# Adding half of each token's expert results by accumulating transfers instead of by VectorE

## The reference

```python
probs = softmax(xt @ w_router)                     # T = 2048 tokens, E = 16 experts
top_w, top_i = top_k(probs, 4)                     # each token has 4 experts
g = silu(xt @ we1) * (xt @ we3)                    # per expert, H = 128
moe_out = sum over the token's 4 experts of  weight * (g @ we2)
shared = silu(xt @ ws1) * (xt @ ws3) @ ws2         # for every token, HS = 512
out = shared / 5 + moe_out * (4 / 5)
x = x + gb * out
```

## Time and profile before

| | us |
|---|---|
| runs | 423.79, 425.45, 425.90; median 425.45 |
| the profiled execution | 426.04 |
| its span (first to last recorded instruction) | 424.3 |
| PE busy | 351.2 (83%) |
| DVE busy | 273.0 (64%) |
| ACT busy | 199.6 (47%) |
| POOL busy | 237.5 (56%) |
| mean granted TensorE clock | 0.92 |

### The profile page before, as it was taken

The page is one execution under the profiler, slowest core; times in us unless marked ns, Lnnn a source line. Parts: engine busy times, 40 slices in busy tenths (PEclk is TensorE's granted clock), DMA queues, the critical chain, the costliest instruction groups (busy, mean ns, idle before and its releaser), DMA issues.

```text
span 424.3 us, 8354 instructions
## 1 busy us (share of the span) xinstructions
PE 351.2 (83%) x2372; PEld 317.7 (75%) x2372; DVE 273.0 (64%) x732; ACT 199.6 (47%) x437; POOL 237.5 (56%) x328
## 2 busy tenths in 40 slices
PE   3988999975999996796655989989999899897552
PEld 1777899974999985675654878878888798786542
DVE  1878988879897564267885554545544455258577
ACT  2446777643657446246351554545545455332020
POOL 1486996546888787877770355655655556600000
PEclk9979999987799998799686999999999999999685
DMA  7154400000011239952223465555546653289411
GB/s 239 59 206 140 131 14 25 14 12 3 15 43 58 85 104 333 355 194 97 99 104 94 127 187 152 151 150 151 174 133 174 171 135 117 87 317 411 177 43 57
DMA packets 54732, 56.65 MB, mean 134 GB/s; under 512 B 17440, under 2 KB 47008, under 8 KB 54688
## 3 DMA queue, kind: packets, MB, share of 16 engines
q1 hardware_dynamic: 46688, 34.34, 27.6%
q0 software_dynamic: 6912, 19.93, 12.5%
q10 hardware_dynamic: 1088, 1.84, 1.3%
HBM read 31.56 MB, written 24.53 MB: 132 GB/s over the span
## 4 chain that ended last, share of the span: by engine, by line
PE 46%; DVE 20%; issue 12%; POOL 11%; ACT 7%; DMA 2%; SPq 1%; DVEq 0%; ACTq 0%; POOLq 0%
PE ps L1408 13%; PE ps L1410 11%; PE ps L1409 11%; POOL xg_rows L551 9%; ACT xT_hi L805 2%; PE ps L1730 2%; DVE y_in L1191 2%; PE ps L1760 2%; DVE gT_lo L1356 2%; DVE act_g L1154 2%; ACT g_hi L674 1%; PE ps L1415 1%; DVE g_lo L1161 1%; POOL hrow L536 1%; DVE xT_lo L1349 1%
## 5 line engine op out<-in xcount | busy, mean ns | idle before, releaser
L578 POOL DMA_INDIRECT y_rows<-y_sb,dest x80 | 76.7, 959 | 72.1 <-ACT y_sb L830 57.6
L551 POOL DMA_INDIRECT xg_rows<-hrow,slot_u x64 | 67.1, 1049 | 19.0 <-issue 17.9
L1408 PE MATMUL ps<-rpool 128*128 128x256 f32 (+3 forms) x228 | 71.7, 314 | 6.5 <-DVE rpool L1232 4.5
L1409 PE MATMUL ps<-rpool 128*128 128x256 f32 (+3 forms) x228 | 68.5, 300 | 0.0
L1410 PE MATMUL ps<-rpool 128*128 128x256 f32 (+3 forms) x228 | 68.4, 300 | 0.0
L1349 DVE TENSOR_TENSOR xT_lo<-ps,xT_hi 128x512 fp32r<-128x512 f32 x40 | 27.7, 692 | 41.9 <-ACT xT_hi L805 41.9
L1408 PEld LDWEIGHTS ps<-rpool 128*128 128x128 f32 x228 | 46.4, 203 | 8.7 <-DVE rpool L1232 4.7
L1408 PE MATMUL ps<-w_hi_routed,xT_hi 128*128 x160 | 49.5, 309 | 4.0 <-issue 4.0
L1409 PEld LDWEIGHTS ps<-rpool 128*128 128x128 f32 x228 | 46.5, 204 | 0.5
L1410 PEld LDWEIGHTS ps<-rpool 128*128 128x128 f32 x228 | 46.2, 203 | 0.6
L1409 PE MATMUL ps<-w_lo_routed,xT_hi 128*128 x160 | 45.7, 286 | 0.0
(11 more groups left out here) (208 smaller groups left out, 963.0 us busy)
## 6 DMA issues: line engine op xcount, KB each, us to landing
xs<-xg_rows SPq DMA_DIRECT2D x80, 128.0 KB
y_in<-y_rows SPq DMA_DIRECT2D x8, 1024.0 KB, 13.3
w_raw_routed<-in_L_ffn_we_dram SPq DMA_DIRECT2D x4, 768.0 KB, 9.3
xg_rows<-empty SPq DMA_DIRECT2D x1, 2304.0 KB, 8.2
x_in<-in_L_attn_x_dram SPq DMA_DIRECT2D x16, 128.0 KB, 2.4
out_dram<-x SPq DMA_DIRECT2D x16, 128.0 KB, 1.8
wmod_sb<-in_L_wmod_dram ACTq DMA_DIRECT2D x3, 512.0 KB, 6.9
w_raw_routed<-in_L_ffn_we_dram SPq DMA_DIRECT2D x1, 1536.0 KB, 14.2
```

The source lines that it names most:

```text
L551: nc.gpsimd.indirect_dma_start(out=xg, out_offset=bass.IndirectOffsetOnAxis(ap=slot_u[:, t, k:k + 1].bitcast(U32), axis=0), in_=hrow[:, t, ...
L578: nc.gpsimd.indirect_dma_start(out=yb, out_offset=bass.IndirectOffsetOnAxis(ap=dest[:, r, i:i + 1].bitcast(U32), axis=0), in_=y_sb[:, r, i ...
L1408: nc.tensor.matmul(dst, w[0], x_[0], start=first, stop=False)
L1409: nc.tensor.matmul(dst, w[0], x_[1], start=False, stop=False)
```

## The change

```diff
-        s_yin = [sem(f"y_in{b}") for b in range(NB)]
+        s_yin, s_yacc = ([sem(f"{n}{b}") for b in range(NB)] for n in ("y_in", "y_added"))
@@ SP's queue
-                    sp.dma_start(y_in[b][:, rows], yb[first:first + BT // 2 * P * TOPK, :].rearrange(
-                        "(t p k) d -> p t k d", p=P, k=TOPK)).then_inc(s_yin[b], 16)
+                    sp.dma_start(y_in[b][:, rows, 0:2], yb[first:first + BT // 2 * P * TOPK, :].rearrange(
+                        "(t p k) d -> p t k d", p=P, k=TOPK)[:, :, 0:2]).then_inc(s_yin[b], 16)
@@ GpSimd's queue, behind the last scatter
+            for r in range(RING):
+                pool.wait_ge(s_back[r], 32 * (NPAIR // RING))
+            for b in SUM_ORDER:
+                pool.wait_ge(s_yin[b], 32)
+                for half in range(2):
+                    first = 1 + (b * BT + half * BT // 2) * P * TOPK
+                    rows = slice(half * BT // 2, (half + 1) * BT // 2)
+                    nc.gpsimd.dma_start(y_in[b][:, rows, 0:2], yb[first:first + BT // 2 * P * TOPK, :].rearrange(
+                        "(t p k) d -> p t k d", p=P, k=TOPK)[:, :, 2:4], accum_op=ALU.add).then_inc(s_yacc[b], 16)
@@ VectorE's queue, add_rows(b)
-                dve.wait_ge(s_yin[b], 32)
-                then(nc.vector.tensor_tensor(y[:, :, 0:2, :], y[:, :, 0:2, :], y[:, :, 2:4, :], ALU.add))
-                summed()
+                dve.wait_ge(s_yacc[b], 32)
                 then(nc.vector.tensor_tensor(y[:, :, 0, :], y[:, :, 0, :], y[:, :, 1, :], ALU.add))
```

## The result

The changed kernel is slower: 432.45 us median of 8 runs (428.25 to 435.48) against 425.49 of 8 runs of the kernel before in the same comparison. The ratio is 1.0138 with a 95% interval of 1.0104 to 1.0173, which on 425.45 us is +5.9 us (+4.4 to +7.4). So it lost 1.4%, clear of the noise and still under 2%. The two profiled executions took 431.37 and 426.04 us, +5.3.

A forecast was written before the change was run, and what follows sets the result against it. VectorE was taken as the bound. Block 0's late rows put unit 11 8.0 us later, three savings of 2.31 give back 6.9, and the clock takes part: +2.75, 428.2 us (428.8 profiled), likeliest case 425.0 to 431.4, overall 421 to 440.

The forecast's parts named there:

- the likeliest case: An accumulating transfer costs two copies and block 0 comes late: middle +2.75 us, range 425.0 to 431.4 us, 44 in 100.
- the rival of three movements: Accumulating costs three or more movements, or GpSimd issues slower than 4.1 us each: 431.5 to 443.5 us, 30 in 100.
- What goes: On VectorE after the last scatter: addition L1191 goes, four times 2.285 us, 2.31 with the small gap behind it.
- Block 0 has no slack: Before the change block 0 was complete at 379.8 us, just as VectorE asked for it at 379.9.
- Two copies for one accumulating transfer: On the DMA engines: two reads for one write count as two copies, 3.0 us for 512 KB.
- The share of the engines: Beside other loads block 0's two accumulating transfers get half to two thirds of the DMA engines, taking 12 or 9 us.
- GpSimd's first addition moves about 1 us later: After block 0's loads land at 377.45 us, GpSimd's first accumulating transfer begins moving at 378.45.
- The clock: TensorE's clock falls before down(11); if it holds or falls at later gaps, block 3's L1202 comes +1.1 or +4.4 us.
- accumulating is nearly a copy: Rival: an accumulating transfer takes 1.5 us per 512 KB; middle -2.4 us, 423.0, break-even about 2.2 us; 26 in 100.
- -8.9: Floor of the change if no rows ever came late and TensorE's clock holds: 416.6 us, practically excluded.

The follow-up runs named there:

- e1: The changed kernel with GpSimd's eight accumulating transfers made plain copies that nobody adds (result incomplete); ratio 1.0044 to before, stage 53.7 us.
- e5: The changed kernel with accumulating transfers for block 0 alone, the other blocks loaded whole and added by VectorE; ratio 1.0304 to before, stage 63.7 us.
- e4: The changed kernel with SP's loads of blocks 2, 1 and 3 held until block 0's accumulating transfers landed; ratio 1.0218 to before, stage 61.7 us.
- e2: The kernel before without VectorE's addition L1191, rows 2 and 3 loaded but left out of the sum; ratio 0.9880, stage 45.8 us.
- e3: The changed kernel with accumulating transfers for blocks 1 and 3 alone, blocks 0 and 2 loaded whole; ratio 0.9957 to before, stage 48.2 us.
- e7: The changed kernel in block order 2, 0, 1, 3, block 2 loaded whole and added by VectorE, the others accumulating; ratio 0.9884 to before, stage 47.1 us.
- e8: Block order 2, 0, 1, 3, block 2 whole, the others accumulating, plus unread matmuls in TensorE's two gaps; ratio 0.9855 to the kernel before, stage 45.6 us.
- e6: The changed kernel with 36, 14 and 10 unread matmuls in TensorE's three gaps; ratio 1.0056 to the kernel before, stage 53.9 us.

## Why the prediction was nearly right

Forecast were 428.8 us for an execution like the profiled one, +2.75; measured were 431.37, and in spans +5.1. The direction and the way of the loss were right, the size was about half of it. The median of 432.45 lies 1 us above the range of the likeliest case (425.0 to 431.4), inside the range of 421 to 440 that covers the rivals as well, and by the number alone it would fit the rival of three movements. What decides between them are the waits and the rates. Taken step by step:

- **What goes** was right: 9.1 us less on VectorE, and at blocks 2, 1 and 3 nothing new was waited for.
- **Block 0 has no slack** was right and decides. Its rows were asked for at +10 and came at +22.3 (forecast 390.2 - 369.87 = +20.3).
- **Two copies for one accumulating transfer** was nearly right. In GB/s it is 208 against 365 for loads in the windows of the result and 385 for e1's copies, a factor of 1.8 to 1.9; 512 KB at 208 GB/s take 2.5 us, not 3.0, against 1.4 for a load. That the pairs landed at about 397, 403 and 409 us (forecast 398.5, 404.5 and 410.5) is partly luck: from block 0's to block 2's it took 5.1 us, and then about 6 a pair because `out`'s stores ran beside them (0.44 of the 1.38 MB that moved between 400 and 406 us).
- **The share of the engines** was put between a half and two thirds, middle taken. From the windows it is (365 - 263) / (365 - 208) = 0.65 for the accumulating side. The rule cited from the Trainium skill, "DMA: Bandwidth & Descriptors", section "Queues, rings and completion order", of turns packet by packet, gives two thirds if such a packet lasts twice as long: this trace agrees, with 329 packets against 345 and 178 ns against 84. In e5, where a load's packet has 4 KB and lasts 159 ns, the same sum gives (395 - 302) / (395 - 208) = 0.50, and the two queues moved 460 and 465 packets: a half, as by the rule.
- **"GpSimd's first addition moves about 1 us later"** is the step that failed. It moved 4.95 us after its issue (377.74 to 382.69), and even in e4, with idle engines, 2.07 us after. The last scatter was 0.34 us earlier than before, so the forecast's 378.45 and 390.2 stand at 378.1 and 389.9 here: the transfer began 4.6 us late. The fewer loads left beside it (0.9 MB at 382.69), the larger share and the shorter transfer gave 2.6 of them back, and block 0 came 2.0 late (391.87).
- **The clock.** I took the middle between clocks that hold and that fall, 2.75 between 1.1 and 4.4. It fell at all three gaps, also at the two that shrank to 4.02 and 3.09 us. That is the end of 4.4, so +1.65. In return the stretches begun at 1.2 GHz were shorter than the 6.5 us taken from the earlier trace rows: unit 13 follows the start of down(11) by 401.77 - 395.14 = 6.6 us, 0.6 of them the silu's, so 6.0 are the matmuls', and it is the same from down(12) to unit 14 (411.73 - 405.12). Two times 0.5 came back.

With the 0.34 us of the last scatter the sum closes: 2.75 + 2.0 + 1.65 - 1.0 - 0.34 = 5.1 us.

The rival **"accumulating is nearly a copy"** was mis-sized in the same two places: it gave -2.4 us and a break-even of 2.2 us per 512 KB, and e1, whose copies took 1.4 us per 512 KB, lost 2.6 us of stage (+0.4% in time). In this order no price of the accumulation down to a copy's pays, because the second trip itself comes too late for block 0. The rival of **three movements or more** is excluded by the 208 GB/s (2.5 us per 512 KB, where it asked for 4.5) and by blocks 2, 1 and 3, which nobody waited for. Two small sums of the prediction are off and change nothing: its shares of 57% and 40% of one range should add up to 100, and the 0.2 us for 1.93 copies leaves out that the shared engines stretch it to 0.3 or 0.4. The floor of **-8.9** was too deep as well: e2 measured -5.3, with the clock falling in the gaps that the saving leaves.

Of the 12.3 us that block 0 came later than before, e1, e4 and the change give the parts: 6.8 are there even alone on the engines (16.9 - 10.1), and 5.4 come from the loads beside it. Put otherwise, 7.7 are the second trip as a copy and 4.5 what accumulating it in packets of 2 KB adds.

What stays open is why GpSimd's first packet starts so late. The runs order the delay by how much of the loads that SP has issued is still to be moved at GpSimd's issue: 2.07 us with nothing or next to nothing left (e4, e3), 2.6 with 1.1 MB (e7, e8), 4.2 to 4.95 with 2.6 to 2.7 MB (e1, e6, the change) and 4.66 with 5.8 MB (e5). In e7 and e8 the loads are all but through when it starts (under 0.1 MB left). In the others 1.6 to 1.8 MB of loads go ahead of it and the rest runs beside it, so it doesn't wait for all loads to end, and more of them than 2.6 MB don't delay it further. The profile doesn't show the queues' inside, and no run varied the loads with this question in view.

## What to carry to other kernels

Work handed to a transfer is gone from the engine but arrives later: here by 12 us at full engines. It pays only for data whose first reader has at least that slack, so look up for each block when it is asked for, hand over the late ones (e3, e7), and arrange the order so that the first block needs no second trip. What an engine saves can be taken back by TensorE's clock in the gaps that arise or remain (e2 gave 5.3 us of 8.9); ask of each forecast gap whether the clock holds, and price the sum with it fallen.

## What was unexpected in the hardware

- Accumulating transfers into SBUF moved 208 GB/s at full engines (186 in e4) where loads of the same 2 KB runs moved 365 and, in e1, 390: a little over half the rate. A packet of 2 KB lasted 178 ns where a load's lasted 84.
- With both queues loaded the engines moved about one packet of one for one of the other (329 and 345 in the change, 460 and 465 in e5), and the share went with the size of the neighbour's packets: 0.63 of the time beside loads of 2 KB, 0.51 beside loads of 4 KB.
- The time from GpSimd's issue to its first packet: 2.07 us alone (e4), 2.6 us with 1.1 MB of loads left (e7, e8), 4.2 to 4.95 us with 2.6 MB or more (e1, e5, e6, the change).
- GpSimd's issue of an accumulating transfer of 256 runs took 1.18 to 1.76 us, of a plain one 0.71 to 0.79 (e1), which went out in half as many packets.
- TensorE's clock fell about 3 us after it stopped in the change (385.2 to 388.3), and in e6 it fell while TensorE was busy again for 1.5 us, after a stop of 1.77. A gap that short is no promise that the clock holds.
